# Layer scores: the preceding tile's last keys read in place, the first scores of a tile in two products

## What is computed

```python
def local_attention(q, k, v):            # 16 heads of 64, window w = 32
    bq, bk, bv = windows of 32 queries, keys, values
    bk2, bv2 = (look(bk), look(bv))      # each window sees the window before it and its own
    mask = (it < jb) | (it > jb + w) | (jb == -1)
    sim = jnp.einsum('bhwie,bhwje->bhwij', bq, bk2) * QK_SCALE
    sim = jnp.where(mask, -jnp.finfo(sim.dtype).max, sim)
    attn = jax.nn.softmax(sim, -1)
    out = jnp.einsum('bhwij,bhwje->bhwie', attn, bv2)

for i in range(DEPTH):                   # 6
    x = attn_layer(shift_tokens(x), Wqkv[i], ...) + x
    x = ffn_layer(shift_tokens(x), ...) + x
```

## Time and profile before

| | |
|---|---|
| three runs | 2070.26 to 2072.15 us, median 2071.22 us |
| profiled execution | 2076.65 us |
| its span, first to last instruction | 2074.8 us |
| mean granted clock of TensorE | 0.975 of full |
| TensorE matmuls | 22192, busy 1915.0 us |
| VectorE | 4021 instructions, busy 1580.7 us |
| ScalarE | 5607 instructions, busy 1597.4 us |
| GpSimd | 1264 instructions, busy 1670.9 us |

### The profile page before, as it was taken

One profiled execution on the slowest core, in us unless ns is written; L12 is line 12 of the kernel. 1 busy time (PEld: TensorE's weight loads), 2 busy tenths in 40 slices (PEclk: granted clock), 3 DMA queues, 4 the chain that ended last, 5 costly groups with the idle time before them and its releaser, 6 DMA issues.

```text
span 2074.8 us, 67230 instructions
## 1 busy us (share of the span) xinstructions
PE 1915.0 (92%) x22192; PEld 1450.5 (70%) x22192; DVE 1580.7 (76%) x4021; ACT 1597.4 (77%) x5607; POOL 1670.9 (81%) x1264
## 2 busy tenths in 40 slices
PE   6996999988999988999988999988999998999987
PEld 4664787764777764777774777774777774777773
DVE  5785888867888866888866788866788876888876
ACT  5884888875888874888874888884888885888873
POOL 3335999957999957999966999976899986999971
PEclk9996999999999999999999999999999999999999
DMA  3001221111211112112112111211211110211110
GB/s 116 14 12 49 54 54 45 45 42 60 59 49 45 45 42 61 48 48 56 47 32 70 49 45 45 53 39 40 78 46 45 45 47 26 58 46 45 45 44 21
DMA packets 44546, 99.42 MB, mean 48 GB/s; under 512 B 7344, under 2 KB 24208, under 8 KB 43504
## 3 DMA queue, kind: packets, MB, share of 16 engines
q1 hardware_dynamic: 44400, 97.59, 18.0%
HBM read 19.59 MB, written 1.05 MB: 10 GB/s over the span
## 4 chain that ended last, share of the span: by engine, by line
PE 72%; issue 11%; POOL 8%; ACT 5%; DVE 3%; DMA 0%; SPq 0%; ACTq 0%; POOLq 0%; DVEq 0%
PE bank L1173 9%; PE bank L1186 8%; PE bank L1200 7%; PE bank L1221 7%; PE bank L1166 7%; PE bank L1202 6%; PE bank L1201 6%; PE bank L1207 6%; PE bank L1157 3%; ACT kT L539 2%; PE bank L1302 2%; POOL rn L329 2%; POOL ropeL L362 2%; POOL tsum L331 2%; PE bank L1213 2%
## 5 line engine op out<-in xcount | busy, mean ns | idle before, releaser
L329 POOL TENSOR_TENSOR rn<-n2c,half_neg 128x8 f32<-128x8 f32 x384 | 636.9, 1658 | 78.6 <-DVE n2c L813 77.8
L501 ACT ACTIVATE prob<-bank,nmax 128x96 f32<-128x96 f32 x1536 | 502.6, 352 | 131.9 <-DVE nmax L763 131.7
L331 POOL TENSOR_TENSOR tsum<-tc_,ts_ 128x512 f32<-128x512 f32 x384 | 489.6, 1275 | 0.0
L334 POOL TENSOR_TENSOR w_nat<-tsum,rn 128x512 f32<-128x512 f32 x384 | 401.3, 1045 | 37.8 <-POOL tsum L331 15.1
L806 DVE TENSOR_REDUCE n<-nat 128x8 f32<-128x512 f32 x384 | 262.4, 683 | 140.1 <-ACT nat L517 128.0
L501 ACT ACTIVATION_READ_ACCUMULATOR prob<-bank,nmax 128x1 f32 x1536 | 333.6, 217 | 0.0
L763 DVE TENSOR_REDUCE nmax<-bank 128x4 f32<-128x384 f32 x384 | 196.3, 553 | 155.4 <-PE bank L1166 147.3
L510 ACT ACTIVATE pT<-bank 96x512 f32<-96x512 f32 x384 | 230.6, 601 | 74.3 <-PE bank L1173 71.9
L1200 PE MATMUL bank<-w_hi,xs 128*128 128x512 f32 x576 | 275.7, 479 | 12.4 <-DVE ts_ L816 9.8
L1173 PE MATMUL bank<-idf,prob 128*96 128x128 f32 x1536 | 246.2, 284 | 43.8 <-ACT kT L539 28.0
L816 DVE TENSOR_TENSOR ts_<-bank,ropeL 128x256 f32<-128x256 f32 x768 | 286.2, 414 | 0.0
(11 more groups left out here) (124 smaller groups left out, 3353.0 us busy)
## 6 DMA issues: line engine op xcount, KB each, us to landing
vspace<-v_nat SPq DMA_DIRECT2D x96, 384.0 KB, 4.0
vspace<-v_nat SPq DMA_DIRECT2D x96, 256.0 KB, 3.4
vspace<-v_nat SPq DMA_DIRECT2D x95, 128.0 KB, 2.2
nat<-w_qkv SPq DMA_DIRECT2D x5, 1536.0 KB, 7.8
wo<-w_o SPq DMA_DIRECT2D x6, 512.0 KB, 4.0
w<-w SPq DMA_DIRECT2D x6, 341.0 KB, 3.1
shared<-w_qkv SPq DMA_DIRECT2D x1, 1536.0 KB, 10.2
w<-w SPq DMA_DIRECT2D x6, 192.0 KB, 3.0
```

What stands on the lines that cost most here:

```text
L329: nc.gpsimd.tensor_tensor(rn[:, r, :], n2c[:, r, :], half_neg[:, 0:8], ALU.pow).then_inc(pool_step, 1)
L331: nc.gpsimd.tensor_tensor(tsum[:, r, :], tc_[:, r, :], ts_[:, r, :], ALU.add).then_inc(pool_step, 1)
L334: nc.gpsimd.tensor_tensor(w_nat[:, r, :].rearrange("p (h d) -> p h d", d=D), tsum[:, r, :].rearrange("p (h d) -> p h d", d=D), rn[:, r, :] ...
L501: last = nc.scalar.activation(prob[:, 4 * b + i, :], SB[b][:, i * SPAN:(i + 1) * SPAN], ACT.Exp, bias=nmax[:, p, 8 * G + 4 * b + i:8 * G + ...
```

## The change

`copy_prev` and its semaphore are gone. The first half of a tile's queries forms its scores in two products for each head: one with the 32 last keys of the other parity's buffer (the tile before), read where they lie, and one with 64 keys of its own. The second half is as before. With it, columns 0 to 31 of `kT` are no longer written in the layers. ScalarE's `heads_T` waits longer before it overwrites keys, since the scores of the next tile now read them too. The mask's constant becomes the more negative, since the first tile of a sequence now reads keys that are not multiplied by zero. The order of the two heads' products is: both heads' first 32 keys, both heads' own 64, both heads' second half.

```diff
-                at_least(eng, s_ready, t * 2 - 2)
+                at_least(eng, s_ready, t * 2 - (2 if j % 2 == 0 else 1 - j // 2))
...
-            def copy_prev(t, n, p):
-
-                at_least(eng, tp_free, t * 4)
-                at_least(eng, s_ready, t * 2 - 2)
-                nc.vector.tensor_scalar(kT[:, p, :, 0:WIN], kT[:, 1 - p, :, P:KEYS], follows[:, bass.ds(n, 1)], None,
-                                        ALU.mult).then_inc(prev_ready, 1)
...
-                    copy_prev(t0, 0, 0)
-                if part == 5:
                     rotary(t0, 0, 3, True)
...
                     if not closing:
-                        copy_prev(t + 1, n + 1, 1 - p)
...
             def scores(t, n, p, G):
 
                 eng.wait_ge(tp_free, t * 4 + (2 * G + 2))
-                eng.wait_ge(prev_ready, t + 1)
...
-                    for half in range(2):
-                        qs, ks = slice(half * HALF, (half + 1) * HALF), slice(half * HALF, half * HALF + SPAN)
-                        for b in range(2):
-                            rows = slice(b * D, (b + 1) * D)
-                            last = nc.tensor.matmul(SB[b][qs, cols], qT[rows, p, g, qs], kT[rows, p, g, ks],
-                                                    start=False, stop=True, skip_group_check=True)
+                    first = slice(i * SPAN, i * SPAN + WIN)
+                    own = slice(i * SPAN + WIN, (i + 1) * SPAN)
+                    for b in range(2):
+
+                        rows = slice(b * D, (b + 1) * D)
+                        nc.tensor.matmul(SB[b][0:HALF, first], qT[rows, p, g, 0:HALF], kT[rows, 1 - p, g, P:KEYS],
+                                         start=False, stop=True, skip_group_check=True)
+                    for b in range(2):
+                        rows = slice(b * D, (b + 1) * D)
+                        nc.tensor.matmul(SB[b][0:HALF, own], qT[rows, p, g, 0:HALF], kT[rows, p, g, WIN:WIN + HALF],
+                                         start=False, stop=True, skip_group_check=True)
+                    for b in range(2):
+                        rows = slice(b * D, (b + 1) * D)
+                        last = nc.tensor.matmul(SB[b][HALF:P, cols], qT[rows, p, g, HALF:P], kT[rows, p, g, HALF:HALF + SPAN],
+                                                start=False, stop=True, skip_group_check=True)
                 last.then_inc(s_ready, 1)
...
-    mask = np.where(seen[None] & ((key >= 0)[None] | (tile > 0)), 0.0, -1e30).transpose(1, 0, 2).astype(f)
+    mask = np.where(seen[None] & ((key >= 0)[None] | (tile > 0)), 0.0, -3.3e38).transpose(1, 0, 2).astype(f)
```

More of the change, by code:

```diff
@@ L165, in build @@
         pool_step, w_ready = sem("pool_step"), sem("w_ready")
-        tp_full, tp_free, prev_ready = sem("tp_full"), sem("tp_free"), sem("prev_ready")
+        tp_full, tp_free = sem("tp_full"), sem("tp_free")
         s_ready, max_ready, p_ready = sem("s_ready"), sem("max_ready"), sem("p_ready")
@@ L1012, in layer @@
                         start(l + 1, 2)
-                    if s == 3 and not last:
-                        start(l + 1, 4)
                     if s == 3 and last:
@@ L1022, in layer @@
                 if not last:
-                    start(l + 1, 5)
-            for part in range(6):
+                    start(l + 1, 4)
+            for part in range(5):
                 start(0, part)
```

## The result

The changed kernel takes 2117.11 us (median of 4 runs, 2111.05 to 2122.77), where the kernel before took 2071.68 us beside it. The ratio is 1.0209, with a 95% interval of 1.019 to 1.0229: 45 us slower, inside the predicted range. Two later comparisons gave 1.0182 (1.0153 to 1.0211) and 1.0184 (1.0165 to 1.0202), that is 38 us. The forecast was 59 us. The execution shown here took 2111.05 us and its span is 2109.2 us, 34.4 us more than the span before; it is the shortest of the four.

A forecast was written before the change was run, and what follows sets the result against it. TensorE was taken to bound the kernel. Removing the copy and moved waits counted zero; 180 calls at 0.33 us added 59.4 us to 2071.2, giving 2131 us, 2.9% slower, range 2104 to 2160.

The forecast's parts named there:

- the price per matmul: Rival, chance 0.06: each matmul in a score call costs a fixed 25.6 ns; 0.41 us a call, 2145 us.
- free loads: Rival, chance 0.06: weight loads in the score calls cost nothing, only streamed columns count; 2071 us.
- the series of groups: Rival, chance 0.15: short product and the four matmuls after it never overlap; 0.47 us a call, 2156 us.
- The loop's larger body: Rival, chance 0.04: TensorE's loop grows by 128 matmuls and loads, 36 passes could stall; 108 us more, 2239 us.
- the last group of a call: Last of four groups in a score call: 281 ns from the start, 118 ns more; the first three 70 ns each.
- my own count of 180 calls: Of 192 score calls, 180 were taken to lengthen the run, at 0.33 us each: 59.4 us.
- TensorE's small waits: One wait less on TensorE, its 0.30 us wait for keys unchanged, the `tp_free` wait as before: zero.
- my twelve hidden ones: Score calls at layer starts hidden behind others: three in layers 1, 2 and 6, one in the other three.
- Its lower end: Bottom of the forecast range, 2104 us: the 0.30 us wait absorbs part of the extra, 90 x 0.36 = 32 us.
- The tile of 16.05 us: Steady tile read from the trace before the change, from one scores(t, 1) to the next; 16.7 us forecast after.

The follow-up runs named there:

- the two runs of 64 matmuls: Changed kernel with short product cut into two of 16 keys, 2198.47 us; changed kernel with the second half's queries split too, 2119.61 us.
- three products: Changed kernel with the short product cut into two of 16 keys, all on the left quarters: 1.0598 of before, 2198.47 us.
- A call of 64 narrow matmuls: Kernel before, copy kept, scores in four blocks of 32 queries by 64 keys instead of two of 64 by 96: 1.0054, 2087.10 us.

## Why the prediction was right, and where it was off

**Right, and shown.** TensorE's own work sets the tile, and the split is the cost: with the copy kept it is as slow. A step on one quarter is 58 ns on average and set by the load, not by streamed columns: 0.23 us a group with 32 or with 8 streamed columns, 0.35 us with six steps, and 37 ns a step where the load has 32 columns. Neither the price per matmul (the two runs of 64 matmuls are 79 us apart), nor free loads, nor the series of groups (1.08 us a call and not 1.29) held. The loop's larger body did not stall: a tile in the loop takes 16.66 us where I had 16.7, and the first call of a pass is as long as the others. Removing the copy alone is worth 4 us (0.07 to 0.31%), 3.0 of them in the loop's passes; I had taken zero.

**The term that was mis-sized** is the last group of a call. I wrote that "the second half starts only behind the long product's first step" and gave it 118 ns more. It starts beside the short product, so the last group costs about 70 ns more like the others, 4 x 70 = 0.28 us. And from the last matmul's start to the next line it now takes 148 ns in place of 173 (medians of 192 calls). The 25 ns fit the 32 columns by which the long product's 64 are fewer than the second half's 96. So a call grew by 0.26 us in all where I had 0.33. With my own count of 180 calls that is 47 us, and with all 192 it is 50 us, against 38 to 45 us measured.

**The rest of the difference.** I had costed TensorE's small waits at nothing. In the loop's passes 144 calls grew by 37 us and the passes by 32. The largest part of these 5 us stands at the end of a pass, where from the last transposes of the probabilities (line 1173) to the mask's products it took 0.86 us before and takes 0.76 now, 3.5 us in 36 passes; the reason isn't shown. Outside the loop 48 calls should add 12 us, or 9 with my twelve hidden ones; the rest of the run grew by 2.3, 11.0 and 3.3 us in three traces. So whether twelve calls hide there can't be told. TensorE's waits for `w_nat`, 5 us less, lie in this part.

**A slip in the range.** Its lower end took the 32 us off 2136.0 us, which is the sum from the profiled execution, and not off the forecast of 2131 us; it should have been 2099. The tile of 16.05 us that I read was also one of the shorter ones; the mean in the loop is 16.22. Neither changes the outcome.

**Wrong on VectorE.** I wrote that its busy time would go down by 86 us. It went down by 48 us with the change, by 27 us where the copy alone was removed, and by 84 us with three products. The copy's long time, 0.94 us beside GpSimd and 0.34 us alone, was a wait for GpSimd; I had read that from the earlier trace rows and then still took the whole time off. Where it meets `w_nat`, the two-input subtraction behind it waits in its place. It cost nothing here, since VectorE waits for TensorE anyway.

## What to carry to other kernels

Before a product is split to save a copy, count the weight loads in a row on each part of the array and not the streamed columns: here each float32 product added on the quarter with the longest row costs two loads of 58 ns, however short it is, while products beside it on other quarters cost 7 us in the whole run where the former cost 86. A copy on an engine that hardly anyone waits for was worth 4 us here and not its 85.9 us of busy time, and taking it out may only hand its wait to the next instruction. Narrower loads do not help as long as wide and narrow ones alternate.

## What was not expected of the hardware

- Matmuls of a later product, on quarters that stand free, are recorded as starting between the two matmuls of an earlier product (721.94 between 721.93 and 721.96). The matmul that frees VectorE, in the second half's product, is no longer the last one to start (722.54); that of the long product starts behind it (722.57).
- Changing between quarters of 64 and strips of 32 columns twice a group makes a group 0.51 us long, where it takes 0.23 us with quarters of 64 alone.
- A call of 64 narrow matmuls starts with 30 in flight and goes on with 23, and in the first call of a loop pass the line behind it starts 0.17 us later than in the others.
- VectorE's wait for GpSimd can move on to the next instruction, where this one meets `w_nat` in turn: 1.27 us for two subtractions that took 0.60 us behind the copy.
